# Two-layer adaLN model on one core: the first eight tiles of the expert layer routed to their two experts through DRAM

## The reference

```
logits = einsum('bsh,eh->bse', tokens, gate_w)            # 16 logits for a token
weights = softmax(logits)
top2_w, top2_idx = top_k(weights, 2)
y = relu(einsum('nh,edh->ned', flat, expert_w) + expert_b)  # (tokens, 16, 128): all experts
sel = take_along_axis(y, flat_idx[:, :, None], axis=1)      # the two that were chosen
out = sum(sel * flat_w[:, :, None], axis=1)
x = x + gb * out
```

## Time and profile before

| | |
|---|---|
| median of 3 runs | 1114.5 us |
| profiled execution | 1114.68 us |
| its span, first to last instruction | 1112.9 us |
| mean granted TensorE clock | 0.990 |
| busy: PE, DVE, ACT, POOL | 1034.9, 870.4, 840.4, 735.5 us |

### The profile page before, as it was taken

How to read it: one execution, slowest core, us unless ns; L and a number is a source line. 1 busy time by engine, 2 the same in 40 slices (tenths; PEclk the granted TensorE clock), 3 DMA queues, 4 the chain that set the end, 5 groups by cost and what they waited for, 6 DMA issues and landing times. The chain is left out here.

```text
span 1112.9 us, 34196 instructions
## 1 busy us (share of the span) xinstructions
PE 1034.9 (93%) x11851; PEld 716.1 (64%) x11851; DVE 870.4 (78%) x2888; ACT 840.4 (76%) x2673; POOL 735.5 (66%) x1184
## 2 busy tenths in 40 slices
PE   6889998799999999898899999998998999999995
PEld 3667764477777776565577777776565598854442
DVE  4999997588888888564788888887685653379998
ACT  5789984699999998433799999997355855478986
POOL 4999995699898897201888988987233220046775
PEclk9999999899999999999999999999999999899999
DMA  7000000112222221321112221221001444000000
GB/s 250 5 3 12 12 3 1 39 40 61 57 54 53 51 49 39 111 73 31 40 39 50 49 49 40 50 49 42 21 1 41 105 122 107 3 8 15 17 20 19
DMA packets 66509, 51.02 MB, mean 46 GB/s; under 512 B 42263, under 2 KB 53443, under 8 KB 66051
## 3 DMA queue, kind: packets, MB, share of 16 engines
q1 hardware_dynamic: 66339, 48.84, 17.3%
HBM read 21.41 MB, written 2.38 MB: 21 GB/s over the span
## 5 line engine op out<-in xcount | busy, mean ns | idle before, releaser
L1259 PE MATMUL psum<-wa_wqkv,wa_hT 128*128 128x512 f32 x384 | 189.0, 600 | 1.3 <-DVE wa_tmp L1124 1.3
L1216 ACT ACTIVATE wa_p<-psum,wa_nb 128x128 f32<-128x128 f32 x512 | 184.7, 403 | 0.0
L1105 POOL TENSOR_TENSOR wa_p<-wa_p,wa_rrs 128x512 f32<-128x512 f32 x128 | 133.4, 1042 | 10.1 <-DVE wa_rrs L1149 10.1
L1140 DVE CUSTOM_DVE_ANT_0 psum<-psum,wa_bias 128x128 f32<-128x128 f32 x512 | 132.5, 322 | 5.8 <-PE psum L1297 5.8
L1216 ACT ACTIVATION_READ_ACCUMULATOR wa_p<-psum,wa_nb 128x1 f32 x512 | 125.0, 244 | 0.0
L1997 ACT ACTIVATE cv_z_ex_yw<-psum,ex_w 128x128 f32<-128x128 f32 x384 | 106.9, 411 | 16.3 <-POOL ex_topf L1829 4.4
L2067 PE MATMUL psum<-ex_wc,ex_hT 128*128 128x512 f32 x256 | 115.8, 600 | 2.4 <-DVE cv_z_ex_yw L1932 1.4
L1081 POOL TENSOR_TENSOR wa_kr<-wa_kr,wa_tmp 128x512 f32<-128x512 f32 x64 | 81.7, 1276 | 41.6 <-DVE wa_tmp L1124 41.6
L1092 POOL TENSOR_TENSOR wa_qr<-wa_qr,wa_rn 128x512 f32<-128x512 f32 x64 | 66.8, 1044 | 56.3 <-ACT wa_rn L1198 56.3
L1226 ACT ACTIVATE wa_pT<-psum 128x512 f32<-128x512 f32 x128 | 78.3, 612 | 31.8 <-PE psum L1273 31.7
L1124 DVE TENSOR_TENSOR wa_tmp<-psum,wa_tabs 128x512 f32<-128x512 f32 x128 | 87.2, 681 | 0.0
(11 more groups left out here) (265 smaller groups left out, 3031.0 us busy)
## 6 DMA issues: line engine op xcount, KB each, us to landing
wa_vm<-wa_v SPq DMA_DIRECT2D x127, 128.0 KB, 2.4
cv_toep<-cv_zpad SPq DMA_DIRECT2D x32, 136.0 KB, 2.9
cv_toep<-cv_zpad SPq DMA_DIRECT2D x16, 264.0 KB, 4.4
wa_tabs<-in_rotations_dram SPq DMA_DIRECT2D x2, 2048.0 KB, 7.9
wa_rows<-y_rows SPq DMA_DIRECT2D x31, 128.0 KB
wa_rows<-y_rows SPq DMA_DIRECT2D x31, 127.0 KB
x_rows<-in_L_attn_x_dram SPq DMA_DIRECT2D x4, 512.0 KB, 5.6
out_dram<-x_rows SPq DMA_DIRECT2D x32, 64.0 KB, 1.5
```

The lines of the kernel that those rows point to most:

```text
L1105: nc.gpsimd.tensor_tensor(p, p, cols_bc(rrs[:, t % 2, r, :], P), ALU.mult)\
L1140: m = nc.vector.tensor_tensor_reduce(out=s, in0=s, in1=edges, scale=-1.0, scalar=MAX_FLOAT, op0=ALU.add, op1=ALU.min, accum_out=nb[:, t % ...
L1216: e = nc.scalar.activation(pr[:, t % 2, r, h, :], sim_bank[r][:, P * h:P * h + P], ACT.Exp, bias=nb[:, t % 2, r, h:h + 1], scale=-1.0, acc ...
L1259: nc.tensor.matmul(bank, hT[:, t % 3, :], wqkv[:, INNER * k:INNER * k + INNER], start=True, stop=True).then_inc(done.sem, 1)
```

## The change

`SPARSE = 8`: tiles 0 to 7 leave the dense loop (now `DENSE` = 24 tiles, tile 8 first). Their tokens go another way, held by the new class `Routed`:

1. Inside the convolution's last steps GpSimd normalizes the eight tiles, TensorE turns them and computes their logits, VectorE finds the two experts of each token. To make room, the output projections of batch row 0 are placed earlier, at parts 1 and 2 of steps 5 and 6.
2. TensorE ranks the 2048 pairs of token and expert by products with a triangular and an all-ones matrix; VectorE works out for each pair a row of a DRAM buffer `ro_hs`, in which each expert's rows begin at a multiple of 128 (`place`), and for each of 32 blocks of 128 rows the column of its expert's weights.
3. GpSimd scatters the normalized tokens to these rows, 16 indirect transfers of 128 rows, four in each of the steps 10 to 13.
4. SyncE waits for all of them and fetches the buffer back as 8 "quads" of 512 rows, and for each block the weights of its expert, from SBUF to SBUF at a column that it reads into a register. Three quads fit. TensorE turns a quad, ScalarE copies it, TensorE multiplies each block by one expert, VectorE applies relu and `gb`, SyncE stores the result to `ro_ys`. Two quads stand in each of the steps 16 to 19.
5. GpSimd gathers each token's two rows, from step 20 on two transfers a step, and VectorE adds them with their weights two steps later. The quads use the six banks and the turning bank together with the dense tiles, in a written order.

The diff, cut to its core:

```diff
+SPARSE = 8
+SCATTER_FROM, SCATTERS_PER = 10, 4
+QUADS_FROM, QUADS_PER = 16, 2
+GATHER_FROM, GATHERS_PER, SUM_LAG = 20, 1, 2
+SGROUPS = SPARSE // 4
+QUADS_OF_ROWS = -(-(2 * SPARSE + NE - 1) // 4)
+    DENSE = TILES - SPARSE
+    tile_of = lambda i: SPARSE + i
...
+        def zero(sp, zeros):
+            rows = ro.hs.rearrange("(r p) e -> p r e", p=zeros.shape[0])
+            sp.dma_start(rows, rows_bc(zeros[:, :], rows.shape[1])).then_inc(ro.zeroed, 16)
+
+        def routed(sp):
+            weights_ready(sp, 0)
+            sp.wait_ge(ro.v_meta, META_DONE)
+            sp.wait_ge(ro.scattered, 16 * 2 * SPARSE)
...
+            def result(q):
+                sp.wait_ge(ro.v_up, q + 1)
+                sp.dma_start(results[q], ro.out_rows[q]).then_inc(ro.stored, 16)
+
+            for q in range(NQ):
+                slot = q % ro.SLOTS
+                if q >= ro.SLOTS:
+                    sp.wait_ge(ro.p_up, q - ro.SLOTS + 1)
+                sp.dma_start(ro.rows_in[slot], rows[q]).then_inc(ro.fetched[slot], 16)
+                for i in range(4):
+                    at = sp.value_load(ro.column[0:1, 4 * q + i:4 * q + i + 1], min_val=0, max_val=(NE - 1) * E)
+                    sp.dma_start(ro.weights_in[slot][:, i, :], wc[:, 0, bass.ds(at, E)])\
+                      .then_inc(ro.fetched[slot], 16)
+                if q >= ro.SLOTS:
+                    result(q - ro.SLOTS)
...
+            def scatter(s):
+                for j, k in scatter_at.get(s, []):
+                    if (j, k) == (0, 0):
+                        gp.wait_ge(ro.zeroed, 16)
+                        gp.wait_ge(ro.v_place, PLACE_DONE)
+                    nc.gpsimd.indirect_dma_start(
+                        out=ro.hs, out_offset=bass.IndirectOffsetOnAxis(ap=ro.pos[:, j, k:k + 1], axis=0),
+                        in_=ro.y[:, j, :], in_offset=None).then_inc(ro.scattered, 16)
+
+            def gather(s):
+                for j in gather_at.get(s, []):
+                    if j == 0:
+                        gp.wait_ge(ro.stored, 16 * NQ)
+                    for k in range(2):
+                        nc.gpsimd.indirect_dma_start(
+                            out=ro.taken(j, k), out_offset=None, in_=ro.ys,
+                            in_offset=bass.IndirectOffsetOnAxis(ap=ro.pos[:, j, k:k + 1], axis=0))\
+                          .then_inc(ro.gathered[j], 16)
...
-                          (residual, UP_LAG + 2)], 0, TILES)
+                          (residual, UP_LAG + 2), step_from(scatter, SCATTER_FROM), step_from(gather, UP_LAG + 2)],
+                         0, DENSE)
...
+        def sums(dve, s):
+            for k in range(2):
+                for j in sum_at.get(s, []):
+                    x = c.x[:, j, :]
+                    dve.wait_ge(ro.v_weight, 3)
+                    dve.wait_ge(ro.gathered[j], 32)
...
+                    nc.vector.scalar_tensor_tensor(out=x, in0=ro.taken(j, k), scalar=ro.w[:, k, j:j + 1], in1=x,
+                                                   op0=ALU.mult, op1=ALU.add).then_inc(ro.v_sum, 1)
...
+            def quad_turn(n):
+                def f(s):
+                    for q in quads_at.get(s, [])[n:n + 1]:
+                        turn_bank_left(pe, "quad", q)
+                        pe.wait_ge(ro.fetched[q % ro.SLOTS], 80 * (q // ro.SLOTS + 1))
+                        for i in range(4):
+                            m = nc.tensor.transpose(h_bank[:, P * i:P * i + P], ro.rows_in[q % ro.SLOTS][:, i, :],
+                                                    c.ident[:, :])
...
+            def quad_up(n):
...
+                        for i in range(4):
+                            m = nc.tensor.matmul(bank[:, P * i:P * i + P], ro.turned[q % 2][:, i, :],
+                                                 ro.weights_in[q % ro.SLOTS][:, i, :], start=True, stop=True)
...
-            return Phase([(by_group(gate), 4), (up(0), UP_LAG), (up(1), UP_LAG), (by_group(turn), 2),
-                          (up(2), UP_LAG), (up(3), UP_LAG)], 0, TILES)
+            return Phase([(by_group(gate), 4), (up(0), UP_LAG), step_from(quad_turn(0), UP_LAG), (up(1), UP_LAG),
+                          step_from(quad_up(0), UP_LAG), (by_group(turn), 2), (up(2), UP_LAG),
+                          step_from(quad_turn(1), UP_LAG), (up(3), UP_LAG), step_from(quad_up(1), UP_LAG)], 0, DENSE)
...
+                on_sync.zero(sp, zeros)
+                on_sync.routed(sp)
                 on_sync.store(sp)
...
+                for s in ro.all:
+                    nc.gpsimd.sem_clear(s)
                 nc.gpsimd.memset(zeros[:, :], 0.0).then_inc(g_zero, 1)
...
+                    if g == PER_B:
+                        on_tensor.ranks(pe, rank)
...
+                    if k == 1:
+                        on_vector.place(dve, rank)
                     residual(g)
+                on_vector.columns_of_weights(dve)
+                on_vector.two_weights(dve)
```

More of the change, by code:

```diff
@@ L1816, in mixing, with fixed @@
                 nc.gpsimd.tensor_copy(mix[:, b, 0:1], c.mod_cols[:, 1, SB, b:b + 1]).then_inc(g_mix, 1)
+        def fixed(gp):
+            nc.gpsimd.memset(ro.ones[...], 1.0).then_inc(ro.g_fixed, 1)
+            nc.gpsimd.memset(ro.count[:, SPARSE, :], 0.0).then_inc(ro.g_fixed, 1)
+            gp.wait_ge(ro.g_fixed, 1)
+            nc.gpsimd.affine_select(out=ro.below[...], in_=ro.ones[...], pattern=[[1, P]], compare_op=ALU.is_gt,
+                                    fill=0.0, base=0, channel_multiplier=-1).then_inc(ro.g_fixed, 1)
+            gp.wait_ge(loaded, 16 * LOADS)
+            nc.gpsimd.tensor_scalar(ro.threshold[...], iota[...], float(P), None, ALU.mult).then_inc(ro.g_fixed, 1)
+            for k in range(4):
+                nc.gpsimd.tensor_scalar(ro.numbers[:, 16 * k:16 * k + 16], iota[0:1, :], float(16 * k), None, ALU.add)\
+                  .then_inc(ro.g_fixed, 1)
@@ L1818, in phase, with routed_rows, residual @@
+        def routed_rows(gp, turned):
+            gp.wait_ge(turned, SGROUPS)
+            nc.gpsimd.memset(ro.y[:, 0:SPARSE, 0:1], 1.0).then_inc(ro.g_rows, 1)
+            for t in range(SPARSE):
+                v_xb.wait(gp, t)
+                nc.gpsimd.tensor_scalar(ro.y[:, t, 1:P], c.x[:, t, 1:P], xs[:, t:t + 1], xb[:, t:t + 1], ALU.mult,
+                                        ALU.add).then_inc(ro.g_rows, 1)
         def phase(gp):
[L1820 to L1822 removed]
+            def residual(i):
+                t = tile_of(i)
+                v_half[3].wait(gp, i)
+                y = total[:, i % RING, :]
@@ L2031, in set_over, with routed_turn, routed_gate @@
             set_done(pe, r)
-        def phase(pe, banks_left):
+        def routed_turn(pe, g, bank):
+            pe.wait_ge(ro.g_rows, 1 + GT * g + GT)
+            for i in range(GT):
+                m = nc.tensor.transpose(bank[:, P * i:P * i + P], ro.y[:, GT * g + i, :], c.ident[:, :])
+            m.then_inc(ro.p_turn, 1)
+        def routed_gate(pe, logits):
+            pe.wait_ge(ro.a_turn, SGROUPS)
+            for t in range(SPARSE):
+                m = nc.tensor.matmul(logits[:, t, :], ro.hT[:, t // GT, t % GT, :], gatec[:, 0, :], start=True,
+                                     stop=True)
+            m.then_inc(ro.p_gate, 1)
@@ new lines, in ranks @@
+        def ranks(pe, rank):
+            pe.wait_ge(ro.g_fixed, FIXED)
+            pe.wait_ge(ro.v_choice, MARKED)
+            flat = rank.rearrange("p t e -> p (t e)")
+            nc.tensor.matmul(flat, ro.below[:, :], ro.count[...].rearrange("p t e -> p (t e)"), start=True, stop=False,
+                             skip_group_check=True)
+            for t in range(SPARSE):
+                m = nc.tensor.matmul(rank[:, t + 1:, :], ro.ones[:, :], rows_bc(ro.count[:, t, :], SPARSE - t),
+                                     start=False, stop=t == SPARSE - 1, skip_group_check=True)
+            m.then_inc(ro.p_rank, 1)
```

401 lines of the change are left out of this document (339 added, 62 removed).

## The result

The changed kernel takes 1156.8 us (median of 4 runs, 1153.5 to 1161.4), the kernel before 1114.4 (4 runs): a ratio of 1.038 with a 95% interval of 1.034 to 1.043. That is slower, as forecast, by 42.3 us where 20 were forecast. The profiled execution took 1161.4 us, 1159.7 of span, and was the slowest of the four.

The account below looks back on a forecast made before the run. In the expert loop TensorE, VectorE and ScalarE were taken to be at their limit together. 1112.9 - 32.1 + 9.4 + 34.2 + 3 + 4.8 = 1132.2 us of span, forecast 1134 us; range leaving out 2 in 10: 1107 to 1165.

Parts of the forecast that it names:

- the routed work in the loop: Expert loop: quads' stage, gathers and sums together add 42.0 us (34.2 + 3 + 4.8).
- What goes: Expert loop: 24 dense tiles in place of 32, eight tiles at 4.01 us each, -32.1 us.
- Ahead of the loop: Last convolution steps to loop start: added transposes, gates, ranking, placing and semaphore clears cost 9.4 us, bounds 4 and 16.
- the prediction's own sign of being wrong: Loop start: the prediction would be wrong if the loop did not start some 9 us later.
- D: The moment of the expert loop's first activation, 979.0 us in the kernel before; forecast loop times count from it.
- The quads: Loop up to tile 10: SyncE's serial fetches and column reads delay it to D+74.3, costing 34.2 us; bounds 18 and 90.
- p: GpSimd's time to issue one indirect transfer (scatter or gather), taken as 1.14 us from the convolution's strided fetches.
- The fifth tile: Loop's tile 4, counted from 0: waits 3.2 us for GpSimd's group weights, due at D+20.2 against D+17.0.
- Gathers and sums: Loop after the quads: gathers on GpSimd in tiles 10 to 17 +3 us, 16 sums on VectorE at 0.30 each +4.8.
- Rival 1: Quads' stage: column reads cost about an issue, a quad every 2.5 us, run 1107.6; decides below some 2.9; chance 0.20.
- Rival 2: GpSimd's scatters and gathers: p at 3 us, tile 10 at D+104, gather steps of 9 us, 1190 us; chance 0.13.
- Rival 3: Quads' stage: waiting TensorE falls to its lower clock, +17 us, 1151; inside the main case's range, no chance of its own.

Follow-up runs that it names:

- e4: Changed kernel with one quad in each of steps 20 to 27 instead of two in each of 16 to 19, gathers from step 28: 1137.2 us.
- e7: Changed kernel without register reads, each weight block fetched from a column fixed in the program (part of the output changed): 1135.8 us.
- e3: Changed kernel without scatters, quads, gathers and sums, only the 24 dense tiles in the loop (output incomplete): 1099.2 us against 1113.4.
- e10: Kernel before plus only the 2 MB zeroing transfer, issued behind the convolution's last fetches to a buffer nothing reads: 1116.4 us, ratio 1.0044.
- e11: Kernel before plus only 31 clears of unused semaphores at the head of GpSimd's last block: ratio 1.0018.
- e2: Changed kernel with ScalarE's scale of group 1 right behind that of group 0 in convolution step 6: 1151.0 us.
- e5: e2 with the 2 MB zeroing transfer of the routed rows' buffer issued at the last block's head: 1150.1 us, ratio 1.035.
- e9: The five edits together, plus early weights and register reads on SyncE, and quads and gathers two steps earlier: 1114.2 us against 1113.1 before, ratio 1.0011.
- e6: Changed kernel with ScalarE copying the ranks to SBUF, so an output projection waits for that copy instead of the placing: 1150.5 us.
- e12: e9 with eight small VectorE operations for expert columns and the two weights moved behind the loop's first step: 1114.2 us, ratio 1.0018.
- The five edits: Changed kernel with clears later, group 1's scale first, zeroing at the head, ranks copied, and quads and gathers later: together 1121.8 us, ratio 1.0079.

## Why the prediction was right and wrong

*Slower, and why in the main:* right. The quads' fetches come one after the other from SyncE, behind 16 scatters, and TensorE stands before them with the dense tiles queued behind. e4 and e7 show it from two sides: the same work later, and the same transfers without reads, take 20 and 18 us away.

*By how much:* 42.3 us and not 20. Two terms of the sum fell short. By the ratios of the changed kernel and e3, with the 32.1 taken as it stands, the part ahead of the loop cost 19 us for 9.4 and the routed work in the loop 56 for 42.0.

*What goes (32.1 us):* nothing speaks against it, but no run measures it alone. e3 runs its 24 tiles at 3.83 us; eight tiles at that pace would be 30.6, and the part ahead of the loop would then be 1.5 us less.

*Ahead of the loop (9.4 us, bounds 4 and 16):* this is the step that failed in its mechanism. e3 prices it at 17.9 to 19.1 us, and the prediction's own sign of being wrong, a loop that does not start some 9 us later, came true: D was 24.5 us late from the block's start on. By landmarks: the head 2.9 to 3.9 (forecast 1 for the clears, with 3 as the bound: GpSimd's earlier groups did not cover them); steps 1 to 5 of the convolution 0.9 to 2.5 more; step 6 8 to 10 more, forecast nothing; step 7 0.3 to 0.5 more, since its turns and gates (3.1 us) stand where projections had stood; loop start 4 to 6 more against 5.1 forecast (5.1 = 1.6 + 2.0 + 1.5). For the loop start the kernel before has 29.1 us in e10 and e11, without the low clock of the earlier trace rows, and against that it is 7 to 8.5 more.

The prediction counted the instructions that were added and left out what the moved ones wait for. The projections, residuals, scales and shifts of batch row 0 came into another written order, and in it one scale stands on ScalarE behind three copies (e2). The second omission is the zeroing transfer: it stands in SyncE's queue in the change, and the sum gives it no price. It holds TensorE up with no wait in the program. In the changed kernel it was under way during the 4.87 us wait, and its pause shows only when e2 takes that wait away. e2 alone takes 2.4 to 4.3 us off step 6, e5 another 4.0, to 11.6; the zeroing moved without e2 was not run.

*The quads (34.2 us, bounds 18 and 90):* right in mechanism, too small in size, 8.7 us by D+83.0 against D+74.3. SyncE began at D+29.2 for 27.7 (a scatter takes 0.96 us and 0.30 to the next, 1.27 in all, for p = 1.14). The eight quads took 47.5 us for 42.2: a read with its issue is 1.18 to 1.25 us and not 1.08, since the prediction took the issue from the stores at 0.33 where this one is 0.6, and the read at 0.75 where it is 0.62. From the last landing to tile 10 it was 1.9 more. Against e3, whose tile 10 starts 27.8 us after tile 3 where the changed kernel's takes 72.7, the stage costs 44.9 us, 10.7 more than forecast. The 2.0 us beyond the 8.7 are the base: the prediction took tile 10 at D+40.1, ten even steps, and without the routed work it starts at D+38.1 (e3).

*The fifth tile* came at D+20.2 as worked out, with 5.6 us of VectorE waiting for GpSimd's weights; that the number is met exactly is luck, since the scatters were dearer than p and began 2.3 us ahead of D. *Gathers and sums:* tile 10 to the last 58.7 for 59.9; against e3's 50.0 the two cost 8.7 where 7.8 were forecast, although a sum is 0.44 us and not 0.30.

*Rivals.* Rival 1 (a quad every 2.5 us, 1107.6) was wrong for this kernel by its own point of decision, 2.9 us a quad: it was 5.4 to 6.6. e9, with the reads out of the way and the other delays lessened, comes to level and not to that gain. Rival 2 (GpSimd at 3 us a transfer): no, 1.27 in the main. Three of the 16 scatters took 1.5 to 1.8 us; the two longest began 0.2 to 0.5 us behind a VectorE halving. Rival 3 (the clock): in part. The granted clock was 0.68 in the first 16 us of the quads, then 1.00 and 0.89:

```profile
1036.00:1052.00 16.00, 7.49 (x31) 4.92 (x32) 3.41 (x6) 4.72 (x16) 6.21 (x16) 0.68 0.32 91
1052.00:1068.00 16.00, 9.26 (x45) 4.93 (x43) 7.96 (x13) 5.78 (x17) 2.54 (x5) 1.00 0.41 115
1068.00:1084.00 16.00, 11.27 (x51) 6.84 (x50) 6.48 (x19) 7.13 (x23) 0.91 (x2) 0.89 0.43 119
```

TensorE was busy for 28 of these 48 us; with that much room the clock did not set the stage. Ahead of the loop it counts, but behind waits, and in step 6 it goes with them (e5).

Open: why the start of the loop after step 7 stays 3.5 to 9 us late in all versions; e6 and e12 each took out one chain there, and another engine's was as late. How much of the head's delay is the lower clock differs between executions.

## What to carry to other kernels

Count a moved instruction by what stands behind it on its engine in the new order, and write that chain down for each engine as carefully as for an added one; here step 6, with a new order of old work and one transfer beside it, lost more (8 to 10 us) than the loop's start with all the ranking and placing (4 to 6). A large transfer is not free because nobody waits for it: put it where the DMA engines and the instruction streams have slack. And where one queue delivers operands in series, place their users as late as the queue's pace says, with its reads and address work done while it idles. The five edits and e9's two took 42 us of loss to none, but not to a gain: the routed blocks then fill TensorE beside the dense ones, and the start of the loop is still late.
